# Mixer and routed experts on one core: step 1 takes group 0 straight to its rows; the last group's choice and half 1's tables move into the expert loop

## The reference, cut to what matters

```python
x = x + _layernorm(mixer(_layernorm(x)))
x = x + _layernorm(experts(_layernorm(x)))

# mixer: a scan per sequence and channel
it, rt = sigmoid(x @ Wi.T + bi), sigmoid(x @ Wr.T + br)
at = exp(-8.0 * softplus(cap_lambda) * rt)
gx = sqrt(1.0 - at ** 2) * (it * x)
h = a * h + g                        # for every step of time

# experts: E = 32, K = 4, H = 128, I = 96
scores = sigmoid(x @ gate_w.T)
topk_ids = top_k(scores + e_bias, K)
topk_w = scores[topk_ids] / sum(scores[topk_ids])
out = sum over the 4 of topk_w * ((silu(x @ w1[e]) * (x @ w3[e])) @ w2[e])
```

## Time and profile before

| | us |
|---|---|
| median of 3 runs | 388.82 (386.69 to 389.78) |
| the profiled execution, by the device | 388.57 |
| its span in the profile | 386.7 |
| busy: TensorE, VectorE, ScalarE, GpSimd | 199.9, 217.9, 200.4, 253.0 |

### The profile page before, as it was taken

The page is one execution under the profiler, slowest core; times in us unless marked ns, Lnnn a source line. Parts: engine busy times, 40 slices in busy tenths (PEclk is TensorE's granted clock), DMA queues, the critical chain, the costliest instruction groups (busy, mean ns, idle before and its releaser), DMA issues.

```text
span 386.7 us, 5981 instructions
## 1 busy us (share of the span) xinstructions
PE 199.9 (52%) x1229; PEld 167.9 (43%) x1230; DVE 217.9 (56%) x945; ACT 200.4 (52%) x493; POOL 253.0 (65%) x292
## 2 busy tenths in 40 slices
PE   1555247436635479999996298999980000000000
PEld 0124224314523359998885198999870000000000
DVE  3256777876877525787543046887446875050524
ACT  6877887797765235665552055656544442020412
POOL 3000077777777777777777777777777777777770
PEclk9996786666565559999999589999996555555555
DMA  4999998111111145776765367888753333132312
GB/s 133 316 293 287 290 291 189 48 54 48 50 54 49 54 141 166 216 226 199 218 187 149 98 164 198 211 215 222 223 146 85 76 93 92 50 79 54 81 48 61
DMA packets 86075, 56.59 MB, mean 146 GB/s; under 512 B 8961, under 2 KB 81953, under 8 KB 86049
## 3 DMA queue, kind: packets, MB, share of 16 engines
q1 hardware_dynamic: 56096, 29.01, 27.0%
q0 software_dynamic: 8192, 16.79, 16.1%
q10 hardware_dynamic: 21760, 10.49, 9.3%
HBM read 25.86 MB, written 30.41 MB: 146 GB/s over the span
## 4 chain that ended last, share of the span: by engine, by line
PE 27%; POOL 16%; issue 8%; DMA 5%; SPq 4%; DVE 1%; ACT 1%; ACTq 0%; POOLq 0%; DVEq 0%
POOL yk L316 16%; PE bank L859 12%; PE bank L876 8%; PE bank L868 4%; PE bank L854 4%; SPq L230 3%; DMA xb<-xs_dram 3%; DMA ys_dram<-yb 1%; DMA yk<-ys_dram,row_ys 1%; SPq L181 1%; DMA xs_dram<-xn_all,row_xs 1%; DVE x_sb L714 0%; ACT L391 0%; ACT xn L440 0%; POOLq L42 0%
## 5 line engine op out<-in xcount | busy, mean ns | idle before, releaser
L305 POOL DMA_INDIRECT xs_dram<-xn_all,row_xs x128 | 126.4, 987 | 83.3 <-DVE row_xs L563 44.6
L316 POOL DMA_INDIRECT yk<-ys_dram,row_ys x128 | 123.2, 962 | 39.0 <-issue 38.7
L859 PE MATMUL bank<-w,xbT 128*128 x320 | 68.7, 339 | 0.4 <-ACT xbT L399 0.4
L674 DVE TENSOR_TENSOR act_a<-silu,bank 128x192 f32<-128x192 f32 x80 | 28.3, 354 | 59.7 <-ACT silu L402 57.9
L859 PEld LDWEIGHTS bank<-w,xbT 128*128 128x128 f32 x320 | 52.6, 198 | 1.2 <-issue 0.8
L399 ACT COPY xbT<-bank 128x256 f32<-128x256 f32 x80 | 29.7, 372 | 41.0 <-PE bank L854 39.3
L876 PE MATMUL bank<-w2s,aT 96*128 x320 | 50.1, 279 | 0.1
L876 PEld LDWEIGHTS bank<-w2s,aT 96*128 96x128 f32 x320 | 42.0, 191 | 1.8 <-issue 1.3
L854 PE MATMUL bank<-ident,xb 128*128 128x128 f32 x160 | 33.8, 289 | 14.4 <-DMA xb<-xs_dram 12.8
L402 ACT ACTIVATE silu<-bank 128x192 f32<-128x192 f32 x80 | 26.4, 330 | 26.0 <-PE bank L859 25.0
L679 DVE COPY yb<-bank 128x256 f32<-128x256 f32 x80 | 33.9, 424 | 7.2 <-PE bank L876 5.2
(11 more groups left out here) (161 smaller groups left out, 384.6 us busy)
## 6 DMA issues: line engine op xcount, KB each, us to landing
xb<-xs_dram SPq DMA_DIRECT2D x160, 64.0 KB
ys_dram<-yb ACTq DMA_DIRECT2D x80, 128.0 KB
xs_dram<-zeros SPq DMA_DIRECT2D x2, 2048.0 KB, 13.5
ys_dram<-zeros SPq DMA_DIRECT2D x2, 2048.0 KB, 11.8
x_sb<-in_L_attn_x_dram SPq DMA_DIRECT2D x8, 256.0 KB, 5.4
xs_dram<-xn_all,row_xs POOLq DMA_INDIRECT x128
yk<-ys_dram,row_ys POOLq DMA_INDIRECT x128, 2.6
out_dram<-x_sb SPq DMA_DIRECT2D x8, 256.0 KB, 2.3
```

The source lines that it names most:

```text
L305: pool.indirect_dma_start(out=xs[h], out_offset=bass.IndirectOffsetOnAxis(ap=row_xs[:, j, k:k + 1], axis=0), in_=xn2_all[:, j, :], in_offs ...
L316: pool.indirect_dma_start(out=yk[h][:, j - h * TH, k, :], out_offset=None, in_=ys[h], in_offset=bass.IndirectOffsetOnAxis(ap=row_ys[:, j, ...
L674: dve.tensor_tensor(act_a[:, o, :, :], silu[:, o, :, :], ps_gu[o][:, 0:4 * I].rearrange("t (b w i) -> t b w i", b=2, w=2)[:, :, 1, :], ALU ...
L859: ins = pe.matmul(ps_gu[o][:, b * 2 * I:(b + 1) * 2 * I], xbT[:, o, b, :], w13[:, bass.ds(expert(i - 1, b), 1), :, :].rearrange("c a w i - ...
```

## The change

**PSUM.** What the choice and half 1's tables need is moved to the columns that `ps_y` (columns 0 to 255 of each bank) leaves free, so that it can live beside the loop.

**Step 1** of the mixer is written out by hand as `second()` on ScalarE, VectorE and TensorE. It takes group 0 (as `c`) on through choice, positions and rows, which were step 2's. Step 2 then has no `e` (`step` leaves out `e == 0`); steps 3 to 8 are as they were, their lines now calls of small functions.

**The last group** (7): its tanh stays ahead of the loop on ScalarE, the rest moves into turns 0 to 3 of loop 0. VectorE's `best`, `take_out` and `chosen` are in `aside`, `positions(7)` and `rows(7)` in a new `ahead(t)`, which stands in a turn ahead of the `ps_y` products (TensorE) and of the `yb` copy (VectorE).

**Half 1's tables** go to turns 5, 7, 9 and 10 of loop 0. Part 2 is split for both halves: `spread` and `unpack_all` (semaphore `v_unpack`) first, `expert_of` and `row_of` in a new part 3. Half 0's part 3 stands behind step 8. Each engine loads half 1's step count between the loops. `packed_rows` and `weigh` move to other turns. TensorE waits explicitly for ScalarE's last reads of the banks ahead of the loop. GpSimd's and SP's programs are the same.

```diff
+        rows_at = ps_pos[:, 2 * P:2 * P + (GT + 1) * E].rearrange("p (j e) -> p j e", e=E)
+        small_at = [ps_tab[:, 0:3], ps_pos[:, 3 * P + 64:3 * P + 67]]
+        spread_at = [ps_tab[:, 3 * P:3 * P + EX], ps_pos[:, 3 * P + 72:3 * P + 72 + EX]]
```

ScalarE's second step and its loop of steps:

```diff
+            def second():
+
+                std_x(2)
+                std_h(0)
+                norm_h(0)
+                norm_x(2)
+                std_1(0)
+                gate_r(1)
+                factor(1)
+                turned_1(0)
+                gate_i(1)
+                score(0)
+                square(1)
+                root(1)
+                turned_x(2)
...
-            for s in range(G + 2):
+            step(0)
+            second()
+            for s in range(2, G + 2):
                 step(s)
 
-            most = [steps_value(act, h) for h in range(HALVES)]
+            most = [steps_value(act, 0)]
             act.preload_act_table(ACT.Silu)
```

VectorE: the second step from `hn` on, the tables, the loop of steps, and what is put into loop 0's turns:

```diff
+            def second():
...
+                add_h(0)
+                stats_1(0)
+                spread_1(0)
+                inverse_1(0)
+                norm_1(0)
+                gate(1)
+                best(0)
+                take_out(0)
+                chosen(0)
+                weight_in(1)
+                rows(0)
+                rows_cast(0)
+                scan(1)
...
                 if part == 2:
                     dve.wait_ge(pe_tab, h + 1)
-                    dve.tensor_copy(expert_of[h][:], ps_tab[0:1, P:2 * P])
-                    dve.tensor_tensor(row_of[h][:], ps_tab[0:1, 2 * P:3 * P], block_row[:], ALU.add)
-                    dve.tensor_copy(unpack_all[h][:], ps_tab[:, 3 * P:3 * P + E]).then_inc(v_tab, 1)
+                    dve.tensor_copy(unpack_all[h][:], spread_at[h][:, 0:E]).then_inc(v_unpack, 1)
+                if part == 3:
+                    dve.wait_ge(pe_own, h + 1)
+                    dve.tensor_copy(expert_of[h][:], owner_at[h])
+                    dve.tensor_tensor(row_of[h][:], moved_at[h], block_row[:], ALU.add).then_inc(v_tab, 1)
...
-            for s in range(G + 2):
+            step(0)
+            second()
+            for s in range(2, G + 1):
                 step(s)
                 if GH + 2 <= s < GH + 5:
                     tables(0, s - GH - 2)
-            for part in range(3):
-                tables(1, part)
+            tables(0, 3)
...
+                    if h == 0 and isinstance(t, int):
+                        ahead(t)
                     dve.tensor_copy(yb[:, (i + 1) % BODY, :, :].rearrange("t b c -> t (b c)"),
...
+            def ahead(t):
+
+                if t == 3:
+                    rows(G - 1)
+                if t in (5, 7, 9):
+                    tables(1, (t - 5) // 2)
+                if t == 10:
+                    tables(1, 3)
+
             def aside(h, t):
...
+                elif t == 0:
+                    best(G - 1)
+                elif t == 1:
+                    take_out(G - 1)
+                    chosen(G - 1)
+                elif t == 2:
+                    packed_rows(0, 0)
+                elif t == 3:
+                    rows_cast(G - 1)
```

TensorE:

```diff
+            def second():
+
+                gate_i(1)
+                turn_x(2)
+                turn_1(0)
+                logits(0)
+                positions(0)
+                gate_r(2)
+                turn_h(1)
...
+                if part == 3:
+                    pe.wait_ge(v_unpack, h + 1)
+                    pe.matmul(owner_at[h], expert_c[:], owner[:], start=True, stop=True)
+                    pe.matmul(moved_at[h], unpack[:], owner[:], start=True, stop=True).then_inc(pe_own, 1)
...
+            pe.wait_ge(a_ti, G)
+            pe.wait_ge(a_tr, G)
+            pe.wait_ge(a_hn, G)
+            pe.wait_ge(a_th, G)
+            pe.wait_ge(v_tab, 1)
```

More of the change, by code:

```diff
@@ L165, in real @@
         def real(g):
-            return 0 <= g < G
+            return g is not None and 0 <= g < G
         def tile(t):
@@ L329, in step, with turned_1 @@
+            def turned_1(g):
+                act.wait_ge(pe_x2T, g + 1)
+                ge(act, pe_logit, g)
+                act.copy(xn2T[:], ps_x2T[:]).then_inc(a_x2T, 1)
             def step(s):
@@ new lines, in take_out, with chosen, rows @@
+            def take_out(e):
+                dve.wait_ge(v_top, e + 1)
+                for j in range(GT):
+                    ins = dve.match_replace(left[:, j, :], top[:, j, :, 0:K], biased[:, j, :], -3e38)
+                ins.then_inc(v_left, 1)
+            def chosen(e):
+                dve.wait_ge(v_left, e + 1)
+                dve.tensor_tensor(mask[:], left[:, :, 0:E], biased[:, :, 0:E], ALU.not_equal).then_inc(v_mask, 1)
+            def rows(e):
+                eh = int(e >= GH)
+                dve.wait_ge(pe_pos, e + 1)
+                dve.tensor_tensor(val_all[:, e * GT:(e + 1) * GT, :], rows_at[:, 0:GT, :], mask[:], ALU.mult).then_inc(v_val, 1)
+                with nc.allow_low_precision(reason="128ths of counts up to 2048 are exact"):
+                    dve.tensor_scalar(seen[eh][:, 0:E], rows_at[:, GT, :], 1.0 / P, None, ALU.mult).then_inc(v_seen, 1)
@@ new lines, in gate, with weight_in, scan @@
+            def gate(g):
+                dve.wait_ge(a_ti, g + 1)
+                dve.scalar_tensor_tensor(out=gated[:], in0=ti[:], scalar=1.0, in1=xnT[:],
+                                         op0=ALU.add, op1=ALU.mult).then_inc(v_gated, 1)
+            def weight_in(g):
+                dve.wait_ge(a_bq, g + 1)
+                dve.wait_ge(v_gated, g + 1)
+                dve.tensor_tensor(gx[:], bq[:], gated[:], ALU.mult).then_inc(v_gx, 1)
+            def scan(g):
+                dve.wait_ge(v_gx, g + 1)
+                ge(dve, pe_h, g)
+                for t in range(0, GC, SEQ):
+                    ins = dve.tensor_tensor_scan(hT[:, t:t + SEQ], at[:, t:t + SEQ], gx[:, t:t + SEQ], 0.0,
+                                                 ALU.mult, ALU.add)
+                ins.then_inc(v_scan, 1)
@@ L549, in step @@
[L549 to L563 removed]
+                    rows(e)
@@ L802, in step @@
[L802 to L814 removed]
+                    turn_x(a)
@@ L836, in _, with ahead @@
                     tables(0, s - GH - 1)
-            for part in range(3):
-                tables(1, part)
+            tables(0, 3)
+            def ahead(t):
+                if t == 3:
+                    positions(G - 1)
+                if t in (5, 7, 9):
+                    tables(1, (t - 5) // 2)
+                if t == 10:
+                    tables(1, 3)
+            pe.wait_ge(a_ti, G)
[3 more added lines that the diff above has]
+            pe.wait_ge(v_tab, 1)
             pe.wait_ge(s_wexp, 48)
             experts = [[pe.alloc_register(f"expert{i}_{b}") for b in range(2)] for i in range(BODY)]
-            most = [steps_value(pe, h) for h in range(HALVES)]
+            most = [steps_value(pe, 0)]
             def expert(i, b):
```

394 lines of the change are left out of this document (230 added, 164 removed).

## The result

| | before | after |
|---|---|---|
| median of 20 runs each, taken together | 388.41 (386.69 to 389.78) | 389.70 (388.19 to 390.85) |
| ratio | | 1.0034, 95% interval 1.0021 to 1.0046 |
| profiled execution, its span | 388.57, 386.7 | 390.45, 388.5 |

The change costs 1.3 us, a third of a per cent. That is little, but with 20 runs of each the interval leaves 1 out. The profiled execution of after is one of the longer ones (0.75 us over its median), so of the 1.9 us between the two traces about 0.6 are chance.

The account below looks back on a forecast made before the run. GpSimd's 256 indirect transfers bound it, two other chains within 3 us. Loop 0's last store: 211.67 + 1.5 + 2.0 = 215.2; first gather 215.4 against 214.41, +1.0; 388.57 + 1.0 = 389.6, range 386 to 392.8.

Parts of the forecast that it names:

- The early start: Step 1 of the mixer: `row_xs(0)` at 38.3, GpSimd starts at 38.6 instead of 49.00, 10.4 us earlier.
- The lateness: Mixer from group 1 on: 4.9 us late (3.9 to 5.4), since group 1's scan stands behind group 0's rows.
- What the early scatters are worth: GpSimd's scatters: 17th at 67.6, 8 of 10.4 us idled away, scatters end 2.4 us earlier (1.9 to 3.4), at 211.7.
- The start of loop 0: First `xb` load at 138.3, 3.5 us later; first expert matmul at 143.2; lateness taken as 1.5 us.
- the two measures: Loop 0's lateness: 2.3 us by half 1's load-to-matmul time, 0.8 by half 1's load-to-store time.
- What lies in the loop: TensorE in loop 0: inserted position and table matmuls add 2.0 to 2.7 us at the low clock; 2.0 taken.
- The cover named for VectorE's middle part: Loop 0: VectorE overruns one turn by under 1 us, but `act_a` and the `ps_y` bank are needed later; cost nothing.
- The gather behind the store: End of loop 0: first gather follows its releasing `ys` store by 0.1 to 0.3 us, at 215.4.
- at most 2.7 us: First gather: moving GpSimd's start alone gives at most this, as loop 0's last store lands 211.67, gather at 214.41.
- The wait moved as said: GpSimd's wait on group 0 becomes one on loop 0's end; loop 1 ends 2.4 us earlier and doesn't bind.
- The first rival: First gather: loop 0's store lands by 212.5, scatters bind, GpSimd keeps its gain: -2.4, 386.2; or -3.4, 385.2; chance 0.20.
- The second: Loop 0: table round trips stop TensorE, 4.9 us in place of 2.0: 392.5, up to 393.8; chance 0.12.

Follow-up runs that it names:

- between_b: Kernel after with half 1's tables between the two loops, group 7's positions and rows still in turn 3; 388.02 against 388.43, ratio 0.9988 to the kernel before.
- step alone: Kernel after with the loop's part taken back: keeps `second()`, group 7's choice and half 1's tables ahead of the loop; 390.57 against 388.43 before, ratio 1.0057.
- hoist_mixer: Kernel before with each group's choice and row casts ahead of the next scan, nothing moved into the loop; 385.96 against 388.43, ratio 0.9940.
- loop alone: Kernel after with the old steps 1 and 2; group 7's choice and half 1's tables in loop 0; 389.03 against 388.43 before, ratio 1.0011.
- hoist_b: Loop alone plus choice and row casts ahead of the next scan from step 2 on; 383.85 against 388.9 before, ratio 0.988; `hoist`, same kernel on a stalled chip, 569.6.

## Why the prediction was right, and where its steps were off

**The early start, right.** First scatter 38.45 (38.6 said), `row_xs(0)` at 37.97 and done at 38.14 (38.3), scan at 38.05 (38.2), `th_all(0)` at 33.68 (33.7), `bq(1)` at 35.78 (35.9). The walk of handovers, each taken from where an engine had waited for just that, held to 0.4 us over 16 us.

**The lateness, right.** Statistics of h(1) at 40.53 (40.9), step 3 at 53.17 (53.5): 4.56 us late, 4.9 said, 3.9 to 5.4 allowed. The cold clock held too: the logits' matmuls of group 0 start at 31.73 in a stretch of granted clock 0.50. Busy time by stretch in after (from:to, length, busy us and counts of TensorE, its weight load, VectorE, ScalarE, GpSimd, then the clock, DMA share and GB/s), at step 1:

```profile
30.00:36.00 6.00, 2.85 (x13) 2.31 (x13) 2.50 (x15) 4.52 (x8) 0.00 (x0) 0.50 0.99 288
```

The Trainium skill ("TensorE: Matmul & The Clock Gate", Part 1) says that an idle array falls back to 1.2 GHz; the row agrees, with 0.50 where TensorE is busy for 2.85 of 6 us.

**What the early scatters are worth, nearly.** The 17th at 67.24 (67.6), idle of 8.06 (8). The scatters ended at 210.26 where 211.7 was said: 3.85 us earlier than before, not 2.4. Of these 2.77 are the 17th scatter (67.24 for 70.01), and 1.07 the way from it to the last, 142.07 us against 143.14 before (213.15 - 70.01), which the forecast took as unchanged. (1.29 us a scatter, not the 1.30 that it read.) It changed nothing, since scatters did not bind.

**The start of loop 0, right.** First load 138.10 (138.3), first product 142.32 for 140.94: 1.4 late, where the two measures had 2.3 and 0.8 and 1.5 was taken.

**What lies in the loop, right in size.** From the first product to the last copy's end loop 0 takes 71.07 us for 68.70: 2.4 more, 2.0 said. Of this 1.65 are the turns with tables, and 0.7 the ramp: 6.78 us from first product to first copy, for 6.06. The ramp is longer since group 7's positions and rows stand in it. Timeline of TensorE (the first positions and the product behind them), then of VectorE (the first of the rows and the first `yb` copy):

```profile
147.76 0.23 PE L953 MATMUL bank<-seen,ones 128*128 128x160 f16 x1
...
148.10 0.66 PE L1108 MATMUL bank<-w2s,aT 96*128 x4
```

```profile
148.80 0.29 DVE L558 TENSOR_TENSOR val_all<-bank,mask 128x128 f32<-128x128 f32 x1 [0.39 <-PE bank L1108]
...
149.10 0.41 DVE L834 COPY yb<-bank 128x256 f32<-128x256 f32 x1
```

They hold up the product by 0.34 us and the copy by 0.30. The clock has little part in it: over the ramp it was 0.61 in after and 0.58 before (rows in the last section). The sum took 2.0 us as matmuls at the low clock. In fact the matmuls take 1.5, at the full clock (0.34 for the positions, 1.2 for the tables), and the rest is time beside them that no term had: 0.2 us for each part of the tables, and the rows ahead of the copy. So the size was partly luck. The cover named for VectorE's middle part held: its turn took 1.54.

**The gather behind the store, mis-sized.** "A gather follows such a release by some 0.1 to 0.3 us once GpSimd is drained" is the term that was mis-sized. Chain of waits in order of time, for `between_b`, from the last copy of loop 0 on:

```profile
209.66 0.44 DVE yb L834
...
210.25 1.86 DMA ys_dram<-yb
212.12 0.02 issue
212.23 0.04 POOLq L317
212.27 0.80 issue
213.07 0.97 POOL yk L321
```

The store lands at 212.11 and the gather starts at 213.07, 0.96 later; 0.80 of it follows the last instruction of GpSimd's queue (POOLq, where the engine's waits stand). From the last copy's end to the first gather it is 2.95 us in after (213.39 to 216.34), 2.95 in the step alone, 2.99 in `between_b`, 2.97 in `hoist_mixer`. That GpSimd is drained is not the reason: in `hoist_mixer` the last scatter ran until 209.09, and the gather still came 0.94 us behind the landing (206.80 + 1.86 = 208.66, by the 1.86 us of the store above). So the first gather stood at 216.34 and not at 215.4, and the profiled execution at 390.45 and not at 389.6. With this term at its true size the sum would have said 390.3. The same term makes the forecast's "at most 2.7 us" for an earlier GpSimd alone too high: 211.67 + 0.95 is 212.6, 1.8 ahead of 214.41. That 389.6 is so near the median of 389.70 is luck in part: the change was forecast at +1.0 us and measured as +1.3 by the medians and +1.9 between the traces, and the forecast started from an execution 0.16 above its median.

**The wait moved as said.** The first gather is released by a `ys` store after 6.07 us of idle time; loop 1, which starts off the scatters (first load 213.88 for 217.13, 3.25 earlier and not 2.4), does not bind: the 65th gather follows the 64th with 0.31. The first rival (scatters bind) falls with that row. The second fell too: TensorE shows no wait for `nblk` or `owner` in loop 0, and a part costs 0.2 us beside its matmuls.

**The rest behind the first gather, nearly constant.** From the first gather to the end it is 174.2 us in before, 174.1 in after, 174.4 in the step alone, 174.0 in the loop alone, 173.6 in `hoist_b`, 174.8 in `hoist_mixer`; it is 175.3 in `between_b`, where 128 gathers take 971 ns each and not 962. That is 1.2 us, which ate most of the 1.3 that its first gather had gained on the kernel before. Why they took longer there was not found out.

## What to carry to other kernels

Three chains arrived within 3 us here, and moving one forward by 10 us at the price of 4.6 us on another was a loss: count what the move makes late before what it makes early, and look first for an order that makes nothing late (here the row casts ahead of the scan: 2.5 us gained alone, 5.0 with the loop's part). Find where an engine's start is released by a small instruction that merely stands behind others in its queue. A part put into a full loop costs its matmuls and a little beside each, here 2.1 us for four; here it brought nothing by itself, and seems to have paid only once GpSimd started earlier.

## What the runs showed of the hardware that was not expected

- An indirect DMA of GpSimd starts 0.94 to 0.96 us behind the landing of the store that it waits for (2.95 to 2.99 us behind the copy that fills the store, in four kernels), whether GpSimd is drained or not; between two queued ones lie 0.30 us.
- When TensorE's clock rises is part of the loop's length. In all seven kernels TensorE was busy without a break from the first product on, and yet the granted clock rose from 0.50 to 1.00 between 2.2 and 5.3 us behind it. The ramp is the time from the first product to the first `yb` copy:

| kernel | group 7's work in the ramp | clock rises, us behind first product | ramp, us |
|---|---|---|---|
| step alone | no | 2.6 | 4.82 |
| `hoist_mixer` | no | 2.9 | 4.98 |
| before | no | 5.1 | 6.06 |
| `hoist_b` | yes | 2.2 | 5.23 |
| loop alone | yes | 4.1 | 6.16 |
| `between_b` | yes | 4.4 | 6.31 |
| after | yes | 5.3 | 6.78 |

In both groups a microsecond more at the lower level makes the ramp about 0.5 us longer, and at equal delay group 7's work makes it some 0.6 longer (an estimate: before with 0.1 added for its delay is 6.16, after 6.78). A loop that comes in later does not have the shorter ramp: after starts later than before and its ramp is longer, also by the clock's part. What sets the delay is not shown. Busy time by stretch, columns as above, over the ramp in after, in before and in the step alone:

```profile
142.32:149.10 6.78, 6.78 (x36) 6.43 (x36) 2.92 (x15) 2.87 (x9) 5.12 (x6) 0.61 0.48 143
```

```profile
140.94:147.00 6.06, 6.06 (x26) 5.81 (x27) 1.01 (x3) 2.48 (x8) 4.70 (x5) 0.58 0.46 135
```

```profile
145.80:150.62 4.82, 4.82 (x26) 4.68 (x27) 1.01 (x4) 2.27 (x8) 3.77 (x4) 0.73 0.50 142
```

- A stalled chip gave the same kernels 570 to 580 us. Of the busy times VectorE's hardly differs (220.0 us in the stalled `hoist`, 218.6 in `hoist_b`); TensorE's is longer (220.0 for 196.3), at a mean granted clock of 0.651 for 0.767. Most of the 190 us are idle stretches of 5 to some 20 us on all engines, and the page puts 20% of the span of `hoist` down to another core or an unknown queue. The stalls came on three chips and not on two others; the cause is open.
